# A decoder of four layers on one core: layer 2's feed forward rewritten, with the key and value projections of layer 3's cross attention in it

## The reference

```python
logits = xf @ Wr.T
topk_vals, topk_idx = jax.lax.top_k(logits, 2)
w = softmax(topk_vals)
sort_idx = argsort(topk_idx.reshape(-1)); rev = sort_idx // 2
chunks = xf[rev].reshape(8, 200, 256)                 # 1600 rows, 200 per expert
h = gelu(einsum('ecd,edf->ecf', chunks, W1))          # W1: 8 x 256 x 1024
eo = einsum('ecf,efd->ecd', h, W2).reshape(1600, 256)
out = zeros.at[rev].add(eo * w.reshape(-1)[sort_idx][:, None])
```

## Time and profile before

| what | time |
|---|---|
| runs of the kernel, median of three | 1692.29 us (1690.16 to 1693.96) |
| the profiled execution | 1695.21 us |
| its span, from the first to the last instruction | 1693.4 us |
| mean granted clock of TensorE in it | 0.890 of 2.4 GHz |
| PE busy | 1402.8 us (83%) |
| DVE, ACT, POOL busy | 792.6, 645.4, 147.6 us |
| `l2_ffn`, first instruction to that of the next sublayer | 1087.9 to 1289.9 us |
| `l3x` cross attention, its first instruction | 1438.2 us |

### The profile page before, as it was taken

How to read it: one execution, slowest core, us unless ns; L and a number is a source line. 1 busy time by engine, 2 the same in 40 slices (tenths; PEclk the granted TensorE clock), 3 DMA queues, 4 the chain that set the end, 5 groups by cost and what they waited for, 6 DMA issues and landing times. The chain is left out here.

```text
span 1693.4 us, 31548 instructions
## 1 busy us (share of the span) xinstructions
PE 1402.8 (83%) x12218; PEld 1060.8 (63%) x12218; DVE 792.6 (47%) x1807; ACT 645.4 (38%) x1704; POOL 147.6 (9%) x167
## 2 busy tenths in 40 slices
PE   7997999979678999769999279719963896999797
PEld 6775668756365778658999146418752575678532
DVE  4666437655545357520000765410005485367575
ACT  3443226533274446413444234302212784246310
POOL 3000010000010100040113000030013000300000
PEclk9999999979755989889999679859986997999899
DMA  5000230001000320267993010243311000520100
GB/s 191 2 1 15 59 64 3 3 29 30 33 2 8 83 37 3 67 217 270 344 344 126 13 32 1 103 151 125 123 31 55 1 2 2 151 38 3 60 1 19
DMA packets 43578, 120.21 MB, mean 71 GB/s; under 512 B 11695, under 2 KB 28205, under 8 KB 37921
## 3 DMA queue, kind: packets, MB, share of 16 engines
q1 hardware_dynamic: 30624, 59.03, 11.6%
q0 software_dynamic: 8256, 55.02, 9.7%
q10 hardware_dynamic: 4560, 4.26, 0.8%
HBM read 95.89 MB, written 11.00 MB: 63 GB/s over the span
## 5 line engine op out<-in xcount | busy, mean ns | idle before, releaser
L692 PE MATMUL wide<-early_kt,early_q 32*100 32x361 f32 x512 | 108.6, 513 | 1.5 <-issue 0.9
L2148 ACT ACTIVATE l1f_hidden<-wide,l1f_pack 128x128 f32<-128x128 f32 x160 | 58.8, 367 | 79.9 <-PE wide L2100 70.3
L2242 DVE TENSOR_TENSOR l1f_out<-summed,l1f_pack 128x256 f32<-128x256 f32 x20 | 8.5, 425 | 155.0 <-PE summed L2108 155.0
L2100 PEld LDWEIGHTS wide<-l1f_rt,l1f_pack 128*128 128x128 f32 x640 | 76.4, 196 | 1.9 <-issue 0.9
L2100 PE MATMUL wide<-l1f_rt,l1f_pack 128*128 128x128 f32 x640 | 76.6, 280 | 0.6 <-ACT l1f_rt L2138 0.6
L2108 PE MATMUL summed<-l1f_pack,l1f_hidden 128*128 128x256 f32 x320 | 72.4, 380 | 0.0
L1064 DVE TENSOR_REDUCE l0x_mx<-wide 100x2 f32<-100x722 f32 x64 | 57.8, 908 | 16.7 <-PE wide L692 16.5
L1064 DVE TENSOR_REDUCE l1x_mx<-wide 100x2 f32<-100x722 f32 x64 | 57.9, 908 | 13.8 <-PE wide L692 13.5
L2108 PEld LDWEIGHTS summed<-l1f_pack,l1f_hidden 128*128 128x128 f32 x320 | 59.4, 191 | 7.1
L1064 DVE TENSOR_REDUCE l3x_mx<-wide 100x2 f32<-100x722 f32 x64 | 57.8, 907 | 12.6 <-PE wide L692 12.6
L3090 PE MATMUL wide<-l3f_we,l3f_xt 128*100 128x512 f32 x128 | 59.0, 616 | 0.8 <-DVE l3f_acc L3158 0.8
(11 more groups left out here) (595 smaller groups left out, 3406.7 us busy)
## 6 DMA issues: line engine op xcount, KB each, us to landing
l2f_w<-l2f_w_dram SPq DMA_DIRECT2D x16, 1024.0 KB, 9.1
ctxt<-ctxt_dram SPq DMA_DIRECT2D x4, 1083.0 KB, 17.2
l1f_sorted_x<-l1f_zeros SPq DMA_DIRECT2D x4, 640.0 KB, 11.5
l1f_rows<-l1f_sorted_x SPq DMA_DIRECT2D x20, 128.0 KB
l1f_sorted_y<-l1f_out ACTq DMA_DIRECT2D x20, 128.0 KB, 9.3
l0f_w<-l0f_w_dram SPq DMA_DIRECT2D x18, 128.0 KB, 2.0
l1f_shared<-l1f_shared_dram SPq DMA_DIRECT2D x1, 2180.0 KB
l3f_we<-l3f_we_dram SPq DMA_DIRECT2D x1, 2048.0 KB
```

What stands on the lines that cost most here:

```text
L692: pe.matmul(wide[0:S, i, 0:SKV], q4[R * i:R * (i + 1), g % 2, b, g // 2, :], kt[R * i:R * (i + 1), g % 2, b, g // 2, 0:SKV], start=True, s ...
L2100: last = pe.matmul(wide[:, f % 4, 0:P], w1_of(w, k, f), rt[:, n % 2, k, :], start=k == 0, stop=k == KC - 1)
L2148: act.activation(hidden[:, f, 0:P], wide[:, f % 4, 0:P], ACT.Gelu, bias=b1_of(pack[:, n % SLOTS, :], f)).then_inc(sem["h_ready"], 1)
L2242: dve.tensor_tensor(out[:, n % 2], summed[:, n % 2, 0:E], b2_of(pack[:, n % SLOTS, :]), ALU.add).then_inc(sem["y_ready"], 1)
```

## The change

`build` now makes a pair of tiles that outlive the feed forward, `Given` (`kd`, `v1`), and loads the context again before `l2_ffn` rather than after `l3_attn`. `l2_ffn` does the following anew:

- SP loads the key weights of layer 3's cross attention, the context in three parts and the value weights ahead of the experts' weights; it waits for `rt_psum` before it loads the next rows and also issues the stores of `sorted_y`.
- POOL clears the padding of `kd` and sets the ones of `v1`.
- TensorE transposes batch b+1 ahead of the logits of batch b; it projects 4 key units between the logits and the counts, 12 key units and the values of two batches between the counts and the first expert, and the values of the other six batches after the last expert. ScalarE copies all of them out.
- VectorE's sums `start` and `base` are made in three steps each by doubling, the two experts' places in one reduction; softmax weights are worked out after the experts.
- The experts are written out one after the other, with the turn of the next always ahead and two buffers for `rt`; the second product waits for each GELU by itself. ScalarE preloads the GELU table.
- Each gathered block has its own semaphore, and its multiply-add follows as it lands, in the order of the gathers.

`cross_attn16` with `fresh` projects only x and queries. `l3_attn` puts `ext`, `share` and `ot` into buffers whose first contents are no longer used.

```diff
+        net.given = Given(net, ctx, "given")
+        with ExitStack() as again:
+            net.context = Context(net, again, "ctxt3")
+            l2_ffn(net)
         l3_attn(net)
-        net.context = Context(net, ctx, "ctxt3")
...
+    order = [("k", b, m) for b in range(B) for m in range(KC)] + [("v", b, i) for b in range(B) for i in range(2)]
+    COUNTED = 4
...
                 load_weights(sp, net, pairs, sem["loaded"])
+                load_weights(sp, net, [(wk[:], dram["l3x_wk"])], sem["wk_loaded"])
+                net.context.load(sp, net, (0,))
+                load_weights(sp, net, [(wv[:], dram["l3x_wv"])], sem["wv_loaded"])
+                net.context.load(sp, net, (1, 2))
+                for e in range(SLOTS):
+                    load_expert(e)
                 sp.wait_ge(sem["scattered"], 16 * TOP * B)
+                for e in range(SLOTS):
+                    load_rows(e)
+                for e in range(NE):
+                    if e + SLOTS < NE:
+                        sp.wait_ge(sem["rt_psum"], e + 1)
+                        load_rows(e + SLOTS)
+                        sp.wait_ge(sem["y_psum"], e + 1)
+                        load_expert(e + SLOTS)
+                    sp.wait_ge(sem["y_ready"], e + 1)
+                    sp.dma_start(sorted_y.rearrange("(e r s) d -> e s r d", r=RT, s=S)[e], out[:, e % 2]).then_inc(stored[e % 2], 16)
...
+                    if b == 0:
+                        pe.wait_ge(sem["loaded"], n_loaded)
+                    else:
+                        logits(b - 1)
+                logits(B - 1).then_inc(sem["l_psum"], 1)
+                pe.wait_ge(sem["wk_loaded"], 16)
+                for what in order[0:COUNTED]:
+                    project(what)
                 pe.wait_ge(sem["both_ready"], 1)
...
+                pe.wait_ge(sem["wv_loaded"], 16)
+                for what in order[COUNTED:2 * (B + AHEAD)]:
+                    project(what)
...
+                turn(0)
+                for e in range(NE):
+                    pe.wait_ge(sem["rt_ready"], e + 1)
...
+                    if e + 1 < NE:
+                        turn(e + 1)
+                    if e >= 1:
+                        pe.wait_ge(sem["y_ready"], e)
+                    for c in range(RT):
                         for f in range(FC):
+                            if c == 0:
+                                pe.wait_ge(sem["h_ready"], e * FC + f + 1)
...
+                for what in order[2 * (B + AHEAD):]:
+                    project(what)
...
+                for i, by in enumerate((1, 2, 4)):
+                    dve.tensor_tensor(start[:, i + 1, by:, :], start[:, i, by:, :], start[:, i, 0:B + 1 - by, :], ALU.add)
+                    if by > 1:
+                        dve.tensor_copy(start[:, i + 1, 1:by, :], start[:, i, 1:by, :])
                     dve.drain()
...
+                for b in range(B):
+                    for k in range(TOP):
+                        dve.wait_ge(gathered[k * B + b], 16)
                         dve.scalar_tensor_tensor(out=net.x[:, b, :], in0=back[:, k * B + b, :], scalar=t.prob[k][:, b, :],
                                                  in1=net.x[:, b, :], op0=ALU.mult, op1=ALU.add)
+                        dve.drain()
...
+                if fresh:
+                    for a in range(HALF):
+                        project(("x", a, 0))
+                    pe.wait_ge(sem["wq_loaded"], 16)
+                    for half in range(2):
                         for m in range(KC):
+                            project(("q", half, m))
+                else:
+                    project_context()
...
+                if not fresh:
+                    values(B - 1)
                 score(1, 0)
+                if not fresh:
+                    pe.wait_ge(sem["v_ready"], B)
```

More of the change, by code:

```diff
@@ L494, in cross_attn16 @@
     GROUPS = ((0, 2), (2, 4), (4, B))
-    ctxt = net.context.tile
+    ctxt = None if fresh else net.context.tile
     kt, q4 = net.tiles.kt, net.tiles.q4
@@ L556, in cross_attn16 @@
         for t in range(B + 1):
-            if t < B:
+            if t < B and not fresh:
                 order += [("k", t, m) for m in range(KC)]
@@ L1101, in _ @@
                 highest(0, 1)
-                if not rope:
+                if not rope and not fresh:
                     values(B - 1)
@@ L2374, in l2_ffn, with rows_of @@
     SLOTS = 4
+    RING = 4
+    V_PARTS = ((0, 2), (2, NCH))
+    AHEAD = 2
+    kd, v1 = net.given.kd, net.given.v1
+    H, D = 16, 16
+    W = D + 1
+    order = [("k", b, m) for b in range(B) for m in range(KC)] + [("v", b, i) for b in range(B) for i in range(2)]
+    unit = {what: u for u, what in enumerate(order)}
+    COUNTED = 4
+    def rows_of(c):
+        return CH if c < NCH - 1 else LAST
     with ExitStack() as ctx:
@@ L2539, in _ @@
-                for e in range(NE - 1):
-                    dve.tensor_tensor(base[:, e + 1:e + 2], base[:, e:e + 1], start[:, B, e:e + 1], ALU.add)
-                    dve.drain()
-                dve.tensor_tensor(rank[:], start[:, 0:B, :], summed[0:S, 1, 0:B * NE].rearrange("s (b e) -> s b e", b=B), ALU.add)
+                    dve.max_index(t.which[:, b, :], t.top[:, b, :], t.logits[:, b, :])
+                dve.tensor_tensor(t.gap[:], t.top[:, :, 1:2], t.top[:, :, 0:1], ALU.subtract).then_inc(sem["gap_ready"], 1)
@@ L2560, in _ @@
[L2560 to L2562 removed]
+                    dve.tensor_tensor(t.hot[k][:], t.whichf[:, :, k:k + 1].broadcast_to([S, B, NE]), t.iota[:], ALU.is_equal)
+                dve.drain()
+                dve.tensor_tensor(both[:], t.hot[0][:], t.hot[1][:], ALU.add).then_inc(sem["both_ready"], 1)
+                dve.wait_ge(sem["count_psum"], 1)
+                dve.tensor_copy(start[:, 0, 1:, :], summed[0:S, 1, B * NE:2 * B * NE].rearrange("s (b e) -> s b e", b=B))
@@ new lines, in _ @@
+                dve.drain()
+                dve.tensor_reduce(place[:], mine[:], X_AX, ALU.add)
+                dve.drain()
+                dve.tensor_copy(placei[:], place[:].rearrange("s k b -> s (k b)")).then_inc(sem["place_ready"], 1)
+                for e in range(NE):
+                    dve.wait_ge(sem["y_psum"], e + 1)
+                    if e >= 2:
+                        dve.wait_ge(stored[e % 2], 16 * (e // 2))
+                    dve.tensor_copy(out[:, e % 2], summed[0:S, :, 0:E]).then_inc(sem["y_ready"], 1)
```

340 lines of the change are left out of this document (191 added, 149 removed).

## The result

The changed kernel takes 1647.77 us (median of four runs, 1646.25 to 1649.54) against 1691.22 for the kernel before beside it: ratio 0.9742, interval 0.9725 to 0.9758, 43.5 us less. The forecast was 1646.0, between 1637 and 1658. The total is right, but one term of the sum is 6 us off, and in the profiled execution an upstream gain and a loss in layer 3's self attention, neither of which I forecast, nearly cancel.

A forecast was written before the change was run, and what follows sets the result against it. TensorE was taken to bound the start of layer 3's cross attention while idle in layer 2's feed forward. Terms 2.5 + 8.0 + 5.4 + 32.1 + 2.1 - 3.8 = 46.3 us gave 1646.0 us, range 1637 to 1658.

The forecast's parts named there:

- A: Layer 2's feed forward, from its start to the row numbers: 2.5 us earlier (bounds 0.5 and 5).
- The counts' wait of 3.1: Inside A: the counts wait for four key units behind the last logits, 4.5 or 1.8 us, middle 3.1.
- the chain of 4.0: Inside A: VectorE's chain from the counts to the cast keeps 4.0 of 5.8 us, 1.8 earlier.
- B: Expert loop: no seam after four experts, second product not waiting for the last GELU; 8.0 us gained (6 to 8.6).
- C: Feed forward's end: each multiply-add follows its own gather, less 0.7 for stretched gathers; 5.4 us gained (3.9 to 6.1).
- The moved work at zero: Key units and values projected under the feed forward's scatter and gather cost zero; 22.7 us if the scatter's cover were gone.
- D: Way to the first score of layer 3's cross attention, no keys projected there: 32.1 us earlier (30 to 34.5).
- E: Layer 3's cross attention: last values no longer stand between the first scores; 2.1 us gained.
- F: Start of layer 3's cross attention loop: slow clock after TensorE's pause for the spreads; costs 3.8 us (2.6 to 4.7).
- Layer 3's self attention at zero: Layer 3's self attention only shares buffers whose users were ordered already: zero change.
- rival 3: Layer 3's cross attention loop never gets its clock back, 4.48 us per step: slower, 1703 us; chance 0.04.
- Rivals 1, 2 and 4: Clock stays up, 1638.8 us (0.13); covers leak, 1654 us (0.16); keys late anyway, between 1670 and old time (0.02).

The follow-up runs named there:

- counted2: Changed kernel with two key units instead of four between the last logits and the counts; 1646.88 us, ratio 0.975.
- ffn_alone: Kernel before with the new `l2_ffn`, without any projection for layer 3 in it; 1673.23 us, ratio 0.989.
- warm: Changed kernel with six unused products of 400 columns in the pause before the first score of layer 3's cross attention; 1655.54 us, ratio 0.9804.
- before_early: Kernel before with layer 3's last batch of values projected ahead of the first score instead of between the first scores; 1700.76 us, ratio 1.0014.
- lift: Changed kernel with six unused products of 400 columns and 128 rows behind the first two scores; 1647.39 us, ratio 0.9703.
- queues: Changed kernel with half of the spreads of layer 3's first queries issued by ScalarE's queue, the other half by SP's; 1651.73 us, ratio 0.9719.
- combo: Changed kernel with two key units before counts, nine gather semaphores, half the first query spreads on ScalarE, keys' second group spread before queries; 1654.08 us, ratio 0.9758.
- ahead5: Changed kernel with three more batches of values projected ahead of the first expert (AHEAD 5 instead of 2); 1643.92 us, ratio 0.9718.

## Why the prediction was right, and where it was not

- *A, 2.5 us expected, 5.1 measured* (stage start to the end of the cast: 28.84 before, 23.70 after). The period of the logits was the term that was too small: I took 1.15 us and it is 0.94, since more of the transposes overlaps; seven periods bring 5.3 instead of 3.8. The rest of the gain, 0.8, lies before and behind them. The counts' wait of 3.1 was right in the main (2.95; 2.4 by `counted2` and 2.5 by `ffn_alone` at the row numbers), and the chain of 4.0 too (3.83).
- *B, 8.0 expected, 7.8 measured* (first product to last copy 112.1 and 104.3). No seam; 12.67 us an expert.
- *C, 5.4 expected, 5.15 measured* (start of the gather to the next stage, 29.92 and 24.77). The two errors in it cancel: the 0.7 for stretched gathers did not come, as the 15 distances between the starts add to 19.5 us in both traces, and 0.9 us came in the gap before the next stage. 14 multiply-adds with two SBUF inputs stood beside gathers of 0.98 to 1.00 us each, so the one gather of 1.13 in the earlier trace rows was no measure for them. By the Trainium skill, GPSIMD Engine Reference, section 1 Specifications, they contend, and C would have been 4.1; here the trace does not bear it out.
- *The moved work at zero* was right as to the covers: 48 records of keys (14.8 us) and 24 of values (5.3) beside the scatter, 72 of values (15.7) from 1234 on beside the last store and the gather, and the experts start as early as without them but for the counts' wait, which is in A (`ffn_alone`). Another 1.2 us of the first expert may or may not belong to it.
- *D, 32.1 expected, 33.8 measured*, the steps as described: SP's eight issues from 1431.99 in 4.95 us, the first score 1.7 us behind them. SP's first issue 12.6 us after the stage's start, where I had 13.9, is most of the difference: the query units ran at a better clock than I took.
- *E and F, a loss of 1.7 us together expected, 7.9 measured.* F is the mis-sized term: 10 us instead of 3.8. I took the recovery from places that are not alike: key units of 128 rows, and two neighbouring steps in layer 1 of which I didn't ask how long the clock had been low before them. In the loop of 32-row products it took 25 us. And E is not separate from F: the values that I removed as a delay were the filling at the loop's start. Of F's 10 us the pause has 2.9 (`warm`), and the bare start the rest, 7.1, or 5.0 net of E's 2.1; `before_early` shows the bare start alone, with 3.8 net, and the 1.2 between the two stay unexplained. These 10 us lie outside the 6 that I allowed F at worst.
- *Layer 3's self attention at zero*: right as to the edits, wrong as to the trace (+8.1). The order of the rivals stands: rival 3 was right in its mechanism, the loop does lose its clock, and wrong in how long: some six slow steps, where it needed 26 to turn the sign. Rivals 1, 2 and 4 did not occur.

The terms of the change come to 18.0 + 25.9 = 43.9 against 46.3: F was 6.2 too good, and A, D and the rest too bad by 3.8. The rest of the profile's 45.6 is gains elsewhere of 8.8 and 0.9 us against a loss of 8.1, in stages that the change leaves alone but for the shared buffers of layer 3's self attention. So the mechanism was right term by term but for E and F, and that the total came within 2 us is in part luck: F's error and the others had opposite signs, and so had the two differences of clock. The bounds of the range are also wider than the text of the terms gives them: it takes 28 for D and 1.5 to 6 for F, where the terms have 30, and 2.6 to 4.7.

## What to carry to other kernels

Work moved into another engine's wait is free as long as the short chain through that wait isn't queued behind it; here four units of it made the row numbers 2.5 us later than none, two 0.1. Before you take work out of the start of a loop, look at what TensorE would wait for without it: the removed 2.1 us held the clock for a loop that loses 1.95 us per step without it. An idle slot on POOL isn't free if VectorE has a short operation on the critical chain beside it. And where transfers fill the DMA engines, a fast TensorE can run out of instructions, which a slower one did not.

## What the runs showed of the hardware that I had not expected

- The clock came up under products of 128 rows within 6 us of the first score (`lift`), and under products of 32 rows at 100% busy only after 25 (changed kernel), 21 (`queues`), 17 (`warm`) and 14 us (`before_early`, `combo`).
- It fell 2.6 to 3.2 us after a wait of 1.0 to 1.2 us for VectorE that followed dense work (`before_early`, `warm`), and in layer 3's self attention right behind 2 us at half load (1366 to 1368). A fall need not come within the pause: in `ahead5` it was at 1.00 over 3.1 us with 0.87 of work and fell when TensorE was busy again, while in the changed kernel it fell 3.7 us into the pause of 9.43.
- VectorE's `tensor_scalar` of 100x8 took 2.12 us (`combo`) and 0.54 us (before) instead of 0.17 and ended with POOL's memset; its multiply-adds and the gathers' issues did not disturb each other.
- TensorE halted for 0.64 to 2.83 us at one place in its instruction list, and 256 records behind it, in three kernels whose loop ran at 2.4 GHz while the DMA engines were full, and went on 1.3 to 1.5 us after a block of 16,384 bytes on queue 8 was in. The other variants of the changed kernel reached that place 1.2 us or more after the block was in, and did not halt.
